# The lead of a conditioned attention layer written out on each engine, with two weight loads at once and sums of squares in four column groups

## What is computed

```python
def _dcoef(weight, style):
    return rsqrt(einsum('oi,bi->bo', square(weight), square(style)) + 1e-8)
x = x * s1[:, None, :]                       # s1, s2: halves of the conditioning vector
x = (x - mean(x)) * rsqrt(var(x) + 1e-5)
q_dc, k_dc, v_dc = (_dcoef(w, s1) for w in (q_weight, k_weight, v_weight))
w_dc, u_dc = _dcoef(w_weight, s2), _dcoef(u_weight, s2)
q = heads(x @ q_weight.T * q_dc);  k = heads(x @ k_weight.T * k_dc)
v_flat = x @ v_weight.T * v_dc * s2
out = softmax(q @ k.T * scale) @ heads(v_flat)
return out @ w_weight.T * w_dc + v_flat @ u_weight.T * u_dc
```

## Time and profile before

| | us |
|---|---|
| runs (three): median, lowest, highest | 4161.56, 4154.67, 4162.0 |
| the profiled execution: its own time | 4159.47 |
| its span, first to last instruction | 4157.7 |
| TensorE busy | 3816.0 (92%) |
| VectorE busy | 3023.7 (73%) |
| ScalarE busy | 1332.5 (32%) |
| GpSimd busy | 1874.0 (45%) |
| mean granted clock of TensorE | 0.949 of 2.4 GHz |

### The profile page before, as it was taken

The page is one execution under the profiler, slowest core; times in us unless marked ns, Lnnn a source line. Parts: engine busy times, 40 slices in busy tenths (PEclk is TensorE's granted clock), DMA queues, the critical chain, the costliest instruction groups (busy, mean ns, idle before and its releaser), DMA issues. The chain is left out here.

```text
span 4157.7 us, 63593 instructions
## 1 busy us (share of the span) xinstructions
PE 3816.0 (92%) x22048; PEld 2324.5 (56%) x22048; DVE 3023.7 (73%) x3166; ACT 1332.5 (32%) x2013; POOL 1874.0 (45%) x1446
## 2 busy tenths in 40 slices
PE   8999749999997899999788999997999939999999
PEld 6777513434344677777566777766777613443434
DVE  4766669999996767777466777753666668999997
ACT  3554411111112433333243333333444511111111
POOL 2555535555553134443313444432455644555554
PEclk9999859999998899999979999998999968999999
DMA  3656655565554122222221222223466665565663
GB/s 118 235 223 234 254 201 172 173 193 177 187 185 138 55 69 77 78 77 64 85 94 59 77 77 77 69 72 126 176 228 232 237 243 168 173 192 177 186 186 122
DMA packets 270513, 619.93 MB, mean 149 GB/s; under 512 B 34112, under 2 KB 36928, under 8 KB 270304
## 3 DMA queue, kind: packets, MB, share of 16 engines
q1 hardware_dynamic: 270304, 617.13, 44.4%
HBM read 380.58 MB, written 236.45 MB: 148 GB/s over the span
## 5 line engine op out<-in xcount | busy, mean ns | idle before, releaser
L1111 DVE CUSTOM_DVE_ANT_0 l0r_g<-l0r_g,l0r_pv,l0r_cf 128x1024 f32<-128x1024 f32 x512 | 674.3, 1339 | 69.9 <-PE l0r_pv L917 46.7
L1111 DVE CUSTOM_DVE_ANT_0 l3r_g<-l3r_g,l3r_pv,l3r_cf 128x1024 f32<-128x1024 f32 x512 | 673.7, 1339 | 70.0 <-PE l3r_pv L917 49.2
L917 PE MATMUL l3r_pv<-l3r_x,l3r_wv 32*128 32x512 f32 x1024 | 261.3, 508 | 23.4 <-POOL l3r_wv L837 15.8
L929 PE MATMUL l0r_py<-l0r_g,l0r_cd 128*32 128x512 f32 x2048 | 282.0, 625 | 0.1
L917 PE MATMUL l0r_pv<-l0r_x,l0r_wv 32*128 32x512 f32 x1024 | 261.9, 511 | 21.9 <-POOL l0r_wv L837 15.8
L929 PE MATMUL l3r_py<-l3r_g,l3r_cd 128*32 128x512 f32 x2048 | 280.0, 620 | 0.1
L917 PEld LDWEIGHTS l0r_pv<-l0r_x,l0r_wv 32*128 32x128 f32 x1024 | 97.4, 187 | 324.1 <-issue 205.2
L917 PEld LDWEIGHTS l3r_pv<-l3r_x,l3r_wv 32*128 32x128 f32 x1024 | 96.9, 187 | 324.1 <-issue 203.3
L1867 POOL TENSOR_TENSOR l1h_st<-l1h_veps,l1h_mhalf 128x1 f32<-128x1 f32 x32 | 17.6, 549 | 349.4 <-DVE l1h_veps L1755 349.4
L1867 POOL TENSOR_TENSOR l2h_st<-l2h_veps,l2h_mhalf 128x1 f32<-128x1 f32 x32 | 17.6, 549 | 349.4 <-DVE l2h_veps L1755 349.4
L101 PE MATMUL l2h_ps_p<-l2h_xh,l2c_wh 128*128 128x512 f32 x384 | 163.9, 427 | 8.8 <-DVE l2h_xl L1781 8.3
(11 more groups left out here) (441 smaller groups left out, 9950.2 us busy)
## 6 DMA issues: line engine op xcount, KB each, us to landing
xhl_s<-l0a_xo SPq DMA_DIRECT2D x128, 512.0 KB, 4.6
l0r_x<-xhl_s SPq DMA_DIRECT2D x128, 512.0 KB, 11.5
xhl_s<-l3a_xo SPq DMA_DIRECT2D x128, 512.0 KB, 4.6
l3r_x<-xhl_s SPq DMA_DIRECT2D x128, 512.0 KB, 11.5
gate_s<-l0a_gate SPq DMA_DIRECT2D x64, 256.0 KB, 2.7
l0r_dx<-dx_s SPq DMA_DIRECT2D x32, 512.0 KB, 13.2
l0r_gate<-gate_s SPq DMA_DIRECT2D x32, 512.0 KB, 13.9
l0r_crow<-feed_s SPq DMA_DIRECT2D x64, 256.0 KB
```

The costliest lines, as they stand in the source:

```text
L917: last = pe.matmul(pv[j % 2][:, h * HALF:(h + 1) * HALF], wv[r, q, 2 * t + j % 2, :], x[r, q, t, j % 2, :], start=True, stop=True)
L929: last = pe.matmul(py[j * JW:(j + 1) * JW, h * HALF:(h + 1) * HALF], cd[:, q, t, j, :], g[:, t, j, h * HALF:(h + 1) * HALF], start=t == 0, ...
L1111: dve._custom_dve(bass.dve_ops.TENSOR_ADD_SAT, out=g[:, t, j, :], in0=g[:, (t - 1) % TS, j, :], in1=pv[j % 2][:, :], s0=cf[:, q, t, 0, j:j ...
```

## The change

The lead is no longer made by `period` at steps -5 to -1: `periods` loses its first loop, and each engine gets a function `lead()`, called once before it, that lists the lead's jobs one by one. SP issues Q's weight ahead of the second tile's loads and K's ahead of the third's. The sums of squares become two steps for every weight: `sum_rows`, four matmuls that write four groups of 32 PSUM rows and don't add to one another, and after a copy to SBUF (`spill`, VectorE) `add_rows`, which adds the four groups with matmuls against a stacked identity (`stack`, made once by VectorE): four matmuls of 32 columns for Q, K, V, one of 512 columns for the other two.

```diff
-def periods(eng, lead, drain, body):
+def periods(eng, drain, body):
-    for d in range(-lead, 0):
-        body(At(0, d))
...
+        stack = ph.sb("stack", [P, B])
+        raw = (pt[:, 0, :, :].rearrange("p h s -> p (h s)"), pt[:, 1, :, :].rearrange("p h s -> p (h s)"))
+        sums = (ps_o, ps_t)
+        early, N = At(0, -1), [At(0, n) for n in range(5)]
...
+            def lead():                       # SP
+                style(N[0]); load(N[0]); load_weight(Q); style(N[1]); load(N[1]); load_weight(K)
+                load(N[2]); style(N[2]); load(N[3]); style(N[3]); load_weight(V)
+                style(N[4]); load(N[4]); load_weight(3); load_weight(4)
...
-            def sum_columns(c):
...
             def sum_rows(c):
                 pe.wait_ge(squared, c + 1)
+                at_least(pe, spilt, c - 1)
                 for k in range(KD):
-                    last = pe.matmul((ps_o, ps_t)[c - 3][0:B, :], cond2[:, KD + k, :], square(c, k), start=k == 0, stop=k == KD - 1)
+                    last = pe.matmul(sums[c % 2][k * B:(k + 1) * B, :], cond2[:, (KD if c > V else 0) + k, :], square(c, k),
+                                     start=True, stop=True)
+                last.then_inc(rowed, 1)
+
+            def add_rows(c):
+                pe.wait_ge(spilt, c + 1)
+                if c > V:
+                    pe.matmul(sums[c % 2][0:B, :], stack[:, :], raw[c % 2], start=True, stop=True).then_inc(summed, 1)
+                    return
+                for m in range(KD):
+                    last = pe.matmul(pd[c][:, m * B:(m + 1) * B], raw[c % 2][:, m * P:(m + 1) * P], stack[:, :], start=True, stop=True)
                 last.then_inc(summed, 1)
...
+            def lead():                       # TensorE
+                turn_x(early, "X0"); turn_x(early, "X1"); sum_rows(Q); turn_x(early, "X2"); add_rows(Q)
+                turn_x(early, "X3"); project(early, Q, "Q", q_mm); sum_rows(K); project(early, K, "K", k_mm)
+                add_rows(K); sum_rows(V); project(early, V, "V", v_mm); add_rows(V)
...
                 project(p, Q, "Q", q_mm)
+                if p.first(0):
+                    add_rows(3)
+                    sum_rows(4)
...
                 project(p, K, "K", k_mm)
+                if p.first(0):
+                    add_rows(4)
...
+            def lead():                       # ScalarE
+                high_weight(Q); normalise(N[0]); square_weight(Q); normalise(N[1]); high_x(early, "X0")
+                high_weight(K); high_x(early, "X1"); normalise(N[2]); square_weight(K); normalise(N[3])
+                high_x(early, "X2"); high_x(early, "X3"); high_weight(V); square_weight(V)
+                take_root(root, dc[:, 0, :, :], 2); keep_k(early); take_root(dc[:, 1, :, :], dc[:, 2, :, :], 3)
+                high_weight(3); square_weight(3)
...
                 exponent(p, 0)
+                if p.first(0):
+                    high_weight(4)
+                    square_weight(4)
...
+            def spill(c):
+                dve.wait_ge(rowed, c + 1)
+                at_least(dve, summed, c - 1)
+                dve.tensor_copy(raw[c % 2], sums[c % 2][:, :]).then_inc(spilt, 1)
...
+            def lead():                       # VectorE
+                dve.reduce_sum(stack[:, :], ident[:, :].rearrange("p (a c) -> p c a", a=P // B), AX.X)
+                statistics(N[0]); statistics(N[1]); low_weight(Q)
+                statistics(N[2]); low_x(early, "X0"); spill(Q); statistics(N[3]); low_x(early, "X1")
+                low_weight(K); low_x(early, "X2"); low_x(early, "X3"); keep_first(); spill(K)
+                low_weight(V); keep_pair(); pair_factor(); keep_q(early); spill(V); keep_skip()
+                skip_factor(); keep_v(early); low_weight(3)
...
+            def lead():                       # GpSimd
+                scale_x(N[0]); scale_x(N[1]); factors(N[0]); scale_x(N[2]); factors(N[1]); scale_x(N[3])
+                factors(N[2]); factors(N[3]); scale_x(N[4])
```

More of the change, by code:

```diff
@@ L1358, in store @@
                 sp.dma_start(rows_of(x_out, n), xr[:, n.mod(4), :]).then_inc(st_ok[n.mod(4)], 16)
+            def lead():
+                style(N[0])
+                load(N[0])
+                load_weight(Q)
+                style(N[1])
+                load(N[1])
+                load_weight(K)
+                load(N[2])
+                style(N[2])
+                load(N[3])
+                style(N[3])
+                load_weight(V)
+                style(N[4])
+                load(N[4])
+                load_weight(3)
+                load_weight(4)
             def period(p):
@@ L1375, in period @@
                     store_factors()
-            periods(sp, LEAD, TAIL, period)
+            lead()
+            periods(sp, TAIL, period)
             for r in range(4):
@@ L1480, in values @@
                     at_least(pe, o_ok, k.count())
+                if k.first(0) and u == 0:
+                    pe.wait_ge(kept, 5)
                 for h in range(HG):
@@ L1491, in turn_v @@
                 if k.first(0):
-                    pe.wait_ge(kept, 5)
+                    pe.wait_ge(kept, 4)
                 for b in range(TB):
@@ L1527, in period @@
                 project(p, V, "V", v_mm)
-            periods(pe, LEAD, TAIL, period)
+            lead()
+            periods(pe, TAIL, period)
         @block.scalar
@@ L1658, in period @@
                     act.activation(froot, flat, ACT.Sqrt).then_inc(rooted, 1)
-            periods(act, LEAD, TAIL, period)
+            lead()
+            periods(act, TAIL, period)
         @block.vector
@@ L1710, in keep_rows @@
                 dve.wait_ge(summed, c + 1)
-                dve.tensor_copy(rows[SLOT[c] - W], (ps_o, ps_t)[c - 3][0:B, :]).then_inc(kept, 1)
+                dve.tensor_copy(rows[SLOT[c] - W], sums[c % 2][0:B, :]).then_inc(kept, 1)
             def add_eps():
@@ L1848, in period @@
                 share(p, 0)
+                if p.first(0):
+                    keep_rows(3)
                 keep_q(p)
+                if p.first(0):
+                    spill(4)
                 share(p, 1)
-                if p.first(-1):
-                    skip_factor()
-                    low_weight(3)
+                if p.first(0):
+                    keep_rows(4)
                 keep_v(p)
-            periods(dve, LEAD, TAIL, period)
+            lead()
+            periods(dve, TAIL, period)
         @block.gpsimd
@@ L1917, in period @@
                 scale_x(p.plus(5))
-            periods(pool, LEAD, TAIL, period)
+            lead()
+            periods(pool, TAIL, period)
 def build(nc, a, out, layers="0123"):
```

122 lines of the change are left out of this document (71 added, 51 removed).

## The result

Seven runs of each kernel: 4157.37 us before (4153.94 to 4163.29), 4168.13 after (4165.34 to 4173.61). The ratio is 1.0023 with an interval of 1.0012 to 1.0033, so the change costs 9.6 us, between 5 and 14 (the two medians are 10.8 apart). The forecast was 4168.0 and +6.4. The profiled execution of after took 4170.27 us, its span is 4168.4.

A forecast was written before the change was run, and what follows sets the result against it. VectorE was taken to set the end from the first product on. Per attention layer 1.0 (D0), 1.3 (period 0) and 0.9 (clock), twice, gave +6.4 us on 4159.5, or 4168 on the runs' scale; range 4153 to 4179.

The forecast's parts named there:

- The first product: TensorE's first product in each attention layer's lead: claimed to start at 1357.6 in layer 1, 10.5 us sooner.
- The chain of x: GpSimd's reordered scales and factors in the lead: factors 0 ends at 1340.7, Q's square at 1343.3, 1.2 us later.
- From there to D0: Lead from first product to first maximum: a serial chain through four engines, 23.1 us plus 0.1 hand-overs, against 11.7 before.
- D0: VectorE's first maximum, after the lead: forecast at 1380.8 in layer 1, 1.0 us later than 1379.8 before the clock term.
- the fall at V's product: TensorE idle about 2.8 us before V's product in the lead, then 1.2 GHz: 0.9 us taken, bounds 0 and 2.8.
- D1: VectorE's second maximum, at 1397.6 before in layer 1; whatever moves it moves the layer's end. Forecast D0 + 19.1 us.
- Period 0: First period after the lead, D0 to D1: 19.1 us against 17.8, 1.3 longer, with two more copies on VectorE.
- rival B: Clock decides: second 1.2 GHz stretch on period 0's V product, slower loads; about +12 us in all, 4173; chance 0.33.
- A: The forecast itself: the leads' sooner product is given back in a serial chain; +2 to +8 us; chance 0.47.
- C: Faster: lead's X chain bound by ScalarE alone, product at 1351.9, D0 at 1375.1; 2 x 4.0 gained, 4153; chance 0.15.
- D: The four column groups run one after another, 3.6 or 7.2 us; 2 x 7.6 more, 4183; chance 0.05.
- Elsewhere nothing: Outside the leads and first periods, no cost; weights 3 and 4 land before use, load 6 at most 3 us.

## Why the prediction was right, and where not

*The first product.* 10.5 sooner was forecast and 11.3 came. On layer 1's lead of the execution that the forecast was worked from, it was 10.7. The chain of x went as worked out: factors 0 was to end 13.3 us after the ident issue and ended 13.4 after it, Q's square 15.9 and 16.0. Q's weight landed 1.0 later than forecast, hidden behind factors 0. Style 2 landed 1.2 earlier than forecast; factors 3's last operation took 2.12 instead of 0.27 us, beside K's low part on VectorE (the row above). The Trainium skill's rule that the two engines block each other (SBUF — State Buffer, "Summary: rules for kernel authors") agrees, and I had applied it to VectorE's low part of period 0 alone: 2.9 forecast, 2.63 measured.

*From there to D0,* layer 1, forecast against measured: Q's product 4.6, 5.42; K's groups 1.05, 1.16; K's product 2.8, 2.9; K's add and the product of the sums 1.3, 1.08; its root 0.35, 0.67; pair factor 2.5, 2.49; Q kept 0.65, 0.83; V's product 2.8 + 0.9 for the clock, 3.99; V's add 0.95, 1.46; epsilon and root 0.75, 0.67; skip factor 2.5, 2.55; V kept 0.65, 0.61; low part 2.2, 2.20. Together 24.0 and 26.03, over all four leads 25.2. The mis-sized terms are mainly those at 1.2 GHz: Q's product ran at 1.2 GHz to its end (one matmul every 0.43 us), and the fall at V's product lasted into V's add, 1.55 in all where I took 0.9 between bounds of 0 and 2.8. The place of the fall was right: V's product began at 0.47 and 0.39 us a matmul and was at 0.63 from its eighth. The granted clock (seventh number) in windows of 1 us of after:

```profile
1371.00:1372.00 1.00, 1.00 (x5) 0.82 (x6) 0.41 (x1) 0.00 (x0) 0.00 (x0) 1.00 0.95 361
1372.00:1373.00 1.00, 1.00 (x5) 0.82 (x4) 0.00 (x0) 0.00 (x0) 0.00 (x0) 0.73 0.03 10
1373.00:1374.00 1.00, 1.00 (x4) 0.82 (x3) 0.00 (x0) 0.00 (x0) 0.00 (x0) 0.50 0.00 0
```

The clock falls while the product runs, after 3.11 us of idle time and 1.5 us of work. D0 was forecast 1.9 later (1.0 + 0.9) and came 1.75 later, since before's other leads were slower than the one that I worked from. On that one alone, layer 1 of the first executions, D0 came 3.6 and D1 5.0 later, where 1.9 and 3.2 were forecast; that the mean over four leads lies so near the forecast is in part luck.

*Period 0.* 1.3 longer forecast, 1.35 measured, and 1.35 given back when that part alone was undone. A second fall came there (weight 3's groups 1.94 us behind 2.68 of idle time), and rival B had feared one, but VectorE covers it; V's product of the period ran at full clock. The 0.7 us that the next period lost on average was not in the forecast.

*The rivals.* A's mechanism is shown by three runs that break the chain in different places (the sums moved, V's add moved, the old sums). B's price was not paid in the leads: it wanted over 1.0 us a layer on top, and they brought none. But the whole, 9.6, lies above A's +2 to +8, between A and B. C did not come by the change, but its D0 was too cautious once the sums move. D is out: 8 instructions in 1.07 us, where the old row sums' 8 took 3.62 at the same clock. In the chances, B and D alone make 0.38, and "slower" was given 0.37 with the upper edge of A in it.

*The step that failed* is "Elsewhere nothing": periods 15 and 16 of layer 1 lose 3.2 to 4.0 us to the stall. Leads 6.2 + stall 3.2 to 4.0 would make 9.4 to 10.2, against 9.6 (5 to 14) measured; but that these two alone meet the total is chance. Means of two executions each, after less before, of layers 1 and 2 together (us, our table):

| stretch | after less before |
|---|---|
| leads and period 0, to D1 | +6.2 |
| D1 to group 15's maximum (0.7 a layer of it up to D2) | +1.6 |
| group 15 to group 31, the stall in layer 1 within it | +3.8 |
| group 31 to the layer's last operation | -3.9 |
| layer 3 and the rest | +1.9 |

The fourth line is mostly layer 2, where that stretch took 55.3 and 55.5 us in before and 52.6 and 52.4 in after, in code that is the same, and 55.4 in the version with the old column sums, whose TensorE program has before's length. So elsewhere there was more than one term, of both signs, 3.4 us net where nothing was forecast. The sum for what was edited held to 0.2, the likeliest class (within 0.2%, chance 0.50) was missed by a hair, the ratio's interval having the bound inside it, and the time, 4168.13, fell on the number forecast only because the median of before lay 4.2 us lower here than in the three runs given.

*What stays open:* why TensorE stands in that block; why the second period's fall of the clock lasts once or twice as long; and why layer 3 takes 2.4 us more in after, and the end of layer 2 3 us less, in code that is the same.

## What to carry to other kernels

An engine relieved of 8 us was not the one that set the end: before splitting a reduction into a faster first pass, a copy and a second pass, follow who waits for the last of the three, and issue the sums ahead of the products that need only their result at the end; here the same instructions gave +10 or -20 us by their order. In a moved lead, look at the stretch behind it too, where a stall that hangs on what the program holds ahead of it can come or go. Compare intervals between landmarks of the same layer, several of them, when a change is as small as the spread of the runs.

## What the runs showed of the hardware that was not expected

- A stall in the middle of a block of score matmuls: TensorE stands 2.0 to 3.5 us (1.7 in one) with no releaser in the profile, once in each profiled execution but those of before and of the old column sums, in layer 1 or, in one version, in layer 2. The two periods take 43.9 us without it, 44.8 in before, up to 48.8 with it.
- After the same idle time of 2.96 us in the second period, the clock fell in every lead, but stayed low twice as long in 13 of 28 (granted 0.64 against 0.81 over 9 us), which cost about 1 us.
- A column sum of 32 matmuls took 7.0 us as the lead's first blocks in before and 3.65 behind a product, at twice the granted clock. I had priced them by the lead's rows alone (0.22 us each); in the new order they are cheap.
- GpSimd's operation on one element per partition took 2.12 us instead of 0.27 when VectorE's low part had begun 0.29 us before it.
